# Local attention: the product taken turned, weights divided ahead of it, and new orders on all engines

## The chip, the cores and the metric

One core of one Trainium2 chip. The metric is the time of one execution in microseconds (us) on the device. The runs of the kernel before took 2020.76, 2023.39 and 2024.77 us, median 2023.39.

## What is computed

The input is 32 sequences of 256 tokens with 128 channels, all in fp32. A linear attention (16 heads of 8) comes first, with normalisation and residual. Then come two layers, each with a local attention and a gated feed-forward. The change touches only the local attention, of which this is the reference, cut to what matters:

```python
h = shift_token(x)                      # second half of the channels from the token before
q, k, v = split(h @ wqkv, 3)            # 8 heads of 64
q = l2norm(q) * qs;  k = l2norm(k) * ksc
q, k = rotary_xpos(q, k)                # t * cos + rotate_half(t) * sin, scaled
sim = einsum('bhwid,bhwjd->bhwij', bq, bk)      # windows of 64, each with the window before
attn = softmax(where(mask, -max, sim))
o = einsum('bhwij,bhwjd->bhwid', attn, bv)
x = x + o @ wo
```

## The kernel before

All of it is one program with an instruction list for each engine, and semaphores between them. Phases follow one another: the linear attention, then for each of two layers the local attention (`t_sync`, `t_pool`, `t_act`, `t_dve`, `t_pe`) and the feed-forward (`f_*`).

The local attention works on tiles of 128 tokens, two to a sequence, 64 in a layer. It is a software pipeline written out by hand. In a slot each engine goes once through its list of steps, and every step names the tile that it works on by its lag: `Tile(l, i, p, s, 2)` is the tile two slots back. So a slot takes in one new tile and works on four at a time (lags 0 to 3); `t_steps` runs the slots, the middle ones in a hardware loop of four slots. The order within a list is the order in the text at the end of each function. Engines run in order; between them `wait_ge` on the semaphores `T[...]` holds a step until its input is there, and `until` holds it until the buffer that it writes has been read.

The way of a tile before: TensorE turns h (L940), ScalarE copies it to hT (L745), TensorE projects k (L954), q (L976) and v (L946) into banks 6 and 7 in turn. VectorE forms the rotary parts of k from the bank (L666 to L669 `straight`, L657 to L664 `swapped`, which is two instructions of half a head each) and adds them (ka, L866). ScalarE copies q to SBUF (L779) and GpSimd does the same three steps for q there (L729, L730, L733). ScalarE squares q and k (L807, L809), VectorE sums the squares per head (ss, L888), and GpSimd raises them to the power -1/2 (`power`: ss L719, rr L722). VectorE multiplies k by it (krot, L856). TensorE turns qrot and krot, ScalarE copies qT and kT (L786, L800), TensorE forms the scores on top of a mask product (L1024 to L1042) in banks 0 and 1. VectorE takes the largest of each row and head (mx, L896) and makes the bias (nb, L900). ScalarE takes eight exponentials of 128x128 (L769), four for even heads (e = 0) and four for odd ones, with rr as scale. TensorE turns the weights (`turn_even`, `turn_odd`), VectorE and ScalarE copy them to pT (L847, L793). The product (`weigh`, L1005, L1006) holds the turned weights stationary, 128x64, and moves the values past them: 64 columns and a 65th of ones, which gives the sum of the weights. `divide` takes the reciprocal of that (L875) and multiplies (L878); TensorE turns the result (`turn_o`), ScalarE copies it to oT (L752), TensorE projects it (L962), VectorE adds the residual (L839). Half the values are wanted on the other 64 partitions, which SP brings there by a DMA (`early_values`, L697). SP also loads hs and yt and stores yn.

TensorE's four-part transposes all stand at L926, in the helper `turn`.

Of the kernel before, what the change touches and what calls it, by code (L numbers as in the profile page):

```python
# [18 lines left out]
ALU = mybir.AluOpType  # L19
# [3 lines left out]
P = 128  # L23
# [54 lines left out]
def build(nc, x, w_qkv, w_out, b_out, rf, wqkv, q_scale, k_scale, wo, ln_g, ln_b, w1, b1, w2, b2, out,  # L78
# [17 lines left out]
    with ExitStack() as ctx:  # L96
# [130 lines left out]
        N_SET = 4 + 1 + 4  # L227
# [31 lines left out]
        def sa(name, shape, dt=F32):  # L259
# [76 lines left out]
        vt = sb("vt", [P, 2, TPB, HEADS, DH + 1])  # L336
        ve = sb("ve", [P, 2, HEADS, DH + 1])
# [3 lines left out]
        pT = sb("pT", [P, 2, UH, P])  # L341
        rl = sb("rl", [P, 2, UH])
        ot = sb("ot", [P, TPB, INNER])
# [302 lines left out]
        class Tile:  # L646

            def __init__(self, l, i, p, s, lag):
                back, self.t = divmod(s - lag, 2)
                self.b = i + back  # L650
# [6 lines left out]
        def swapped(on, src, dst, l, a, t):  # L657

            s4 = src.rearrange("p (h c d) -> p h c d", c=2, d=DH // 2)
            d4 = dst.rearrange("p (h c d) -> p h c d", c=2, d=DH // 2)  # L660
            for c in range(2):
                sin = ltab[:, l, a + 1, t, 32 * c:32 * c + 32].unsqueeze(1).broadcast_to([P, HEADS, DH // 2])
                m = on.tensor_tensor(d4[:, :, c, :], s4[:, :, 1 - c, :], sin, ALU.mult)  # L663
            return m  # L664

        def straight(on, src, dst, l, a, t):  # L666
            cos = ltab[:, l, a, t, :].unsqueeze(1).broadcast_to([P, HEADS, DH])
            return on.tensor_tensor(dst.rearrange("p (h d) -> p h d", d=DH), src.rearrange("p (h d) -> p h d", d=DH),  # L668
                                    cos, ALU.mult)  # L669

        def t_sync(sp, l, i, p):
# [19 lines left out]
            def early_values(X):  # L691
# [3 lines left out]
                until(sp, T["o_ps"], 4 * X.n - 4)  # L695
# [8 lines left out]
            early_values(Tile(l, i, p, 0, 1))  # L704
# [4 lines left out]
            early_values(Tile(l, i, p, 1, 1))  # L709

        def t_pool(pool, l, i, p, s):

            def power(X):
# [7 lines left out]
                until(pool, T["po"], X.x - 3)  # L721
                nc.gpsimd.tensor_tensor(rr[:, r, :], ss[:, r, :], half_neg[:], ALU.pow).then_inc(T["rr"], 1)  # L722

            def rotate_q(X):
# [4 lines left out]
                swapped(nc.gpsimd, qraw[:, X.t, :], m2q[:], l, 0, X.t)  # L729
                straight(nc.gpsimd, qraw[:, X.t, :], m1q[:], l, 0, X.t).then_inc(T["qm"], 1)  # L730
# [3 lines left out]

            power(Tile(l, i, p, s, 1))
            rotate_q(Tile(l, i, p, s, 0))

        def t_act(act, l, i, p, s):

# [7 lines left out]
            def turned_o(X):  # L747
                if not X.live:
                    return
                act.wait_ge(T["oT_ps"], X.x + 1)  # L750
                until(act, T["w_ps"], X.x - 1)
                nc.scalar.copy(oT[:, X.t].rearrange("p j n -> p (j n)"), turn_bank(s, 0)[:]).then_inc(T["oT"], 1)  # L752

            def values(X):
                if not X.live:
                    return
                act.wait_ge(T["v_ps"], X.x + 1)
                until(act, T["o_ps"], 2 * X.x - 4)
                nc.scalar.copy(vt[:, X.p, X.t, :, 0:DH],
                               project_bank(s, 0)[:].rearrange("p (h d) -> p h d", d=DH)).then_inc(T["v"], 1)  # L760

            def exps(X, e):
# [4 lines left out]
                for j in range(UH):  # L767
# [6 lines left out]
            def queries(X):  # L774
                if not X.live:
                    return
                act.wait_ge(T["q_ps"], X.x + 1)
                until(act, T["qrot"], X.x - 1)
                nc.scalar.copy(qraw[:, X.t, :], project_bank(s, 2)[:]).then_inc(T["q"], 1)  # L779

            def turned_q(X):
                if not X.live:
                    return
                act.wait_ge(T["qT_ps"], X.x + 1)
                until(act, T["s_ps"], X.x - 1)
                nc.scalar.copy(qT[:, X.t].rearrange("p j n -> p (j n)"), turn_bank(s, 2)[:]).then_inc(T["qT"], 1)  # L786

            def turned_odd(X):
                if not X.live:
                    return  # L790
                act.wait_ge(T["po_ps"], X.x + 1)
                until(act, T["o_ps"], 2 * X.x)
                nc.scalar.copy(pT[:, 1].rearrange("p j n -> p (j n)"), turn_bank(s, 3)[:]).then_inc(T["pTo"], 1)  # L793

            def turned_k(X):
# [4 lines left out]
                nc.scalar.copy(kT[:, X.p, :, 1 - X.t, :], turn_bank(s, 4)[:].rearrange("p (j n) -> p j n", n=P)  # L800
                               ).then_inc(T["kT"], 1)

            def squares(X):
                if not X.live:
                    return
                until(act, T["ss"], X.x)
                nc.scalar.activation(sq[:, 0:INNER], project_bank(s, 2)[:], ACT.Square).then_inc(T["qs"], 1)  # L807
                act.wait_ge(T["km"], X.x + 1)
                nc.scalar.activation(sq[:, INNER:], project_bank(s, 1)[:], ACT.Square).then_inc(T["ks"], 1)  # L809
# [12 lines left out]
        def t_dve(dve, l, i, p, s):  # L822

            def rotate_k(X):
                if not X.live:
                    return
                dve.wait_ge(T["k_ps"], X.x + 1)
                until(dve, T["ka"], X.x)
                straight(nc.vector, project_bank(s, 1), m1k[:], l, 2, X.t)
                swapped(nc.vector, project_bank(s, 1), m2k[:], l, 2, X.t).then_inc(T["km"], 1)  # L830

            def residual(X):
                if not X.live:
                    return
                if X.t == 0:
                    dve.wait_ge(T[f"y_in{X.p}"], 16 * half_count(X.n))
                    until(dve, T[f"out{X.p}"], 16 * (half_count(X.n) - 1))
                dve.wait_ge(T["w_ps"], X.x + 1)
                nc.vector.tensor_tensor(yn[:, X.p, X.t, :], yt[:, X.p, X.t, :], bank[4][:, 0:D], ALU.add  # L839
                                        ).then_inc(T["yn"], 1)  # L840

            def turned_even(X):
                if not X.live:
                    return
                dve.wait_ge(T["pe_ps"], X.x + 1)
                until(dve, T["o_ps"], 2 * X.x - 1)
                nc.vector.tensor_copy(pT[:, 0].rearrange("p j n -> p (j n)"), turn_bank(s, 1)[:]  # L847
                                      ).then_inc(T["pTe"], 1)

            def norm_k(X):  # L850
                if not X.live:
                    return
                dve.wait_ge(T["rr"], X.x + 1)
                dve.wait_ge(T["ka"], X.x + 1)
                until(dve, T["kT_ps"], X.x - 1)
                nc.vector.tensor_tensor(krot[:, X.t, :].rearrange("p (h d) -> p h d", d=DH),  # L856
                                        ka[:].rearrange("p (h d) -> p h d", d=DH),
                                        rr[:, 2 * X.p + X.t, HEADS:].unsqueeze(2).broadcast_to([P, HEADS, DH]),
                                        ALU.mult).then_inc(T["krot"], 1)

            def add_k(X):
                if not X.live:
                    return
                dve.wait_ge(T["km"], X.x + 1)
                until(dve, T["krot"], X.x)
                nc.vector.tensor_tensor(ka[:], m1k[:], m2k[:], ALU.add).then_inc(T["ka"], 1)  # L866

            def divide(X):
                if not X.live:
                    return  # L870
                o = psA[2].rearrange("p (e n) -> p e n", e=2)[:, :, 0:UH * (DH + 1)].rearrange(
                    "p e (j d) -> p e j d", d=DH + 1)
                dve.wait_ge(T["o_ps"], 2 * X.x + 2)
                until(dve, T["o"], X.x)
                nc.vector.reciprocal(rl[:], o[:, :, :, DH]).then_inc(T["rl"], 1)  # L875
                dve.wait_ge(T["rl"], X.x + 1)
                until(dve, T["oT_ps"], X.x - 1)
                nc.vector.tensor_tensor(ot[:, X.t].rearrange("p (j e d) -> p e j d", e=2, d=DH), o[:, :, :, 0:DH],  # L878
# [501 lines left out]
```

## Time and profile before

| | |
|---|---|
| runs shown | 2020.76, 2023.39, 2024.77 us (median 2023.39) |
| the profiled execution, its own time | 2025.17 us |
| its span in the profile | 2023.4 us |
| mean granted TensorE clock | 0.98 |
| PE busy | 1821.6 us (90%) |
| DVE busy | 1387.1 us (69%) |
| ACT busy | 1290.3 us (64%) |
| POOL busy | 1207.2 us (60%) |

PE is TensorE (PEld its weight loads), DVE VectorE, ACT ScalarE, POOL GpSimd, SP the queue that issues the DMAs. An engine's busy time is what its instructions last; a PE at 90% isn't at its peak, since matmuls are pipelined. "L926" is line 926 of the kernel. What stands behind `<-` in brackets is what ended an idle time of the engine. A row with x2 and more merges that many instructions of one kind in a row. In a projection or a product each fp32 matmul shows as two.

### The profile page before, as it was taken

The numbers are of one execution on the slowest core, as the hardware profiler recorded it, in microseconds if no ns is written. First come the engines' busy times: TensorE is split into PE (matmuls) and PEld (weight loads), VectorE is DVE, ScalarE is ACT, GpSimd is POOL, SyncE is SP. The second block draws the span as 40 slices with busy tenths as digits, with TensorE's granted clock in tenths as the row PEclk, the third lists the DMA queues.
The fourth block names the chain that finished last, engine by engine and source line by source line (L and its number), as shares of the span: only waits on it lengthen the run. The fifth ranks groups of instructions, "written<-read, shape, count | busy, mean of one in ns | idle before, by whom it ended". The sixth has DMA issues, their size and how long they took to land.

```text
span 2023.4 us, 54270 instructions
## 1 busy us (share of the span) xinstructions
PE 1821.6 (90%) x18884; PEld 1223.0 (60%) x18884; DVE 1387.1 (69%) x3157; ACT 1290.3 (64%) x2692; POOL 1207.2 (60%) x1143
## 2 busy tenths in 40 slices
PE   4999999689999999999969988999999999996997
PEld 3666666356666666666635545666666666663554
DVE  3777777567777777777746746777777777774887
ACT  4888888467777777777732216777777777773221
POOL 0323323277777777777722217777777777773454
PEclk9999999899999999999989988999999999998999
DMA  4111111111111111111113221111111111112342
GB/s 100 53 49 44 51 48 46 50 30 36 36 34 34 31 38 35 31 34 32 35 46 82 78 60 30 36 32 37 36 31 34 31 39 34 31 32 53 98 113 81
DMA packets 209334, 94.31 MB, mean 47 GB/s; under 512 B 90818, under 2 KB 200300, under 8 KB 209260
## 3 DMA queue, kind: packets, MB, share of 16 engines
q1 hardware_dynamic: 209260, 93.35, 17.7%
q8 instruction: 43, 0.70, 0.1%
q14 instruction: 31, 0.25, 0.0%
HBM read 51.03 MB, written 25.23 MB: 38 GB/s over the span
## 4 chain that ended last, share of the span: by engine, by line
PE 56%; ACT 17%; issue 10%; POOL 4%; DVE 4%; SPq 4%; DMA 4%; ACTq 0%; POOLq 0%; DVEq 0%
PE banks L926 17%; ACT pr L769 8%; PE banks L976 5%; PE banks L946 5%; PE banks L1024 4%; ACT kT L800 4%; PE banks L1005 4%; DMA f_y<-y_d 3%; PE banks L561 3%; PE banks L510 3%; PE banks L1042 3%; PE banks L575 3%; SPq L1094 3%; PE banks L1034 2%; ACT L472 2%
## 5 line engine op out<-in xcount | busy, mean ns | idle before, releaser
L663 POOL TENSOR_TENSOR m2q<-qraw,ltab 128x256 f32<-128x256 f32 x256 | 244.7, 976 | 251.4 <-ACT qraw L779 229.3
L722 POOL TENSOR_TENSOR rr<-ss,half_neg 128x16 f32<-128x16 f32 x128 | 374.2, 2923 | 19.1 <-POOL ss L719 17.1
L769 ACT ACTIVATE pr<-banks,nb,rr 128x128 f32<-128x128 f32 x1024 | 371.7, 477 | 0.8 <-DVE nb L900 0.6
L926 PE MATMUL banks<-ident,pr 128*128 128x128 f32 x1024 | 161.4, 280 | 59.1 <-ACT pr L769 56.4
L1157 ACT ACTIVATE f_g<-banks,b_s 128x512 f32<-128x512 f32 (+1 forms) x96 | 65.8, 686 | 225.2 <-PE banks L1241 224.2
L888 DVE TENSOR_REDUCE ss<-sq 128x16 f32<-128x1024 f32 x128 | 156.1, 1220 | 30.8 <-ACT sq L809 27.9
L1006 PE MATMUL banks<-vt,pT 128*64 128x65 f32 x2048 | 173.9, 228 | 0.0
L962 PEld LDWEIGHTS banks<-wo_s,oT 128*128 128x128 f32 x1024 | 134.0, 192 | 63.2 <-issue 45.8
L733 POOL TENSOR_TENSOR qrot<-m1q,m2q 128x512 f32<-128x512 f32 x128 | 162.9, 1273 | 14.2 <-POOL m1q L668 8.2
L745 ACT COPY hT<-banks 128x128 f32<-128x128 f32 x128 | 34.0, 266 | 214.5 <-PE banks L940 214.5
L926 PEld LDWEIGHTS banks<-ident,pr 128*128 128x128 f32 x1024 | 113.7, 141 | 85.8 <-ACT pr L769 85.8
L668 POOL TENSOR_TENSOR m1q<-qraw,ltab 128x512 f32<-128x512 f32 x128 | 163.6, 1278 | 0.0
L372 POOL TENSOR_SCALAR a_ve<-a_mv 128x2 f32<-128x2 f32 x96 | 21.1, 220 | 231.4 <-DVE a_mv L383 228.4
L896 DVE TENSOR_REDUCE mx<-banks 128x8 f32<-128x1024 f32 x128 | 155.5, 1215 | 3.1 <-PE banks L1034 3.1
L875 DVE RECIPROCAL rl<-banks 128x8 f32<-128x8 f32 x128 | 26.6, 208 | 181.8 <-PE banks L1006 181.8
L1034 PE MATMUL banks<-kT,qT 64*64 64x128 f32 x2048 | 141.4, 278 | 0.0
L1006 PEld LDWEIGHTS banks<-vt,pT 128*64 128x64 f32 x2048 | 138.4, 137 | 0.0
L668 DVE TENSOR_TENSOR m1k<-banks,ltab 128x512 f32<-128x512 f32 x128 | 88.6, 692 | 72.2 <-PE banks L954 72.2
L962 PE MATMUL banks<-wo_s,oT 128*128 128x128 f32 x1024 | 135.5, 276 | 2.7 <-ACT oT L752 2.7
L946 PE MATMUL banks<-wqkv_s,hT 128*128 128x512 f32 x256 | 133.9, 605 | 3.0 <-ACT sq L809 3.0
L954 PE MATMUL banks<-wqkv_s,hT 128*128 128x512 f32 x256 | 134.3, 607 | 0.8 <-ACT hT L745 0.8
L847 DVE COPY pT<-banks 128x512 f32<-128x512 f32 x128 | 88.5, 692 | 67.4 <-PE banks L926 67.3
(130 smaller groups left out, 4677.0 us busy)
## 6 DMA issues: line engine op xcount, KB each, us to landing
ve<-vt SPq DMA_DIRECT2D x128, 130.0 KB, 2.2
hs<-y_d SPq DMA_DIRECT2D x128, 64.0 KB, 1.9
yt<-y_d SPq DMA_DIRECT2D x64, 128.0 KB, 2.1
y_d<-yn SPq DMA_DIRECT2D x64, 128.0 KB, 2.0
f_h<-y_d SPq DMA_DIRECT2D x128, 64.0 KB, 2.0
f_y<-y_d SPq DMA_DIRECT2D x64, 128.0 KB, 2.2
xa<-in_L_attn_x SPq DMA_DIRECT2D x32, 128.0 KB, 2.1
xr<-in_L_attn_x SPq DMA_DIRECT2D x32, 128.0 KB, 2.3
```

The source lines that it names most:

```text
L663: m = on.tensor_tensor(d4[:, :, c, :], s4[:, :, 1 - c, :], sin, ALU.mult)
L668: return on.tensor_tensor(dst.rearrange("p (h d) -> p h d", d=DH), src.rearrange("p (h d) -> p h d", d=DH), cos, ALU.mult)
L722: nc.gpsimd.tensor_tensor(rr[:, r, :], ss[:, r, :], half_neg[:], ALU.pow).then_inc(T["rr"], 1)
L733: nc.gpsimd.tensor_tensor(qrot[:, X.t, :], m1q[:], m2q[:], ALU.add).then_inc(T["qrot"], 1)
L769: a = nc.scalar.activation(pr[:, e, j, :], bank[e][:, j * P:(j + 1) * P], ACT.Exp, bias=nb[:, X.t, UH * e + j:UH * e + j + 1], scale=rr[:, ...
L888: nc.vector.tensor_reduce(ss[:, 2 * X.p + X.t, :], sq[:].rearrange("p (h d) -> p h d", d=DH), AX.X, ALU.add).then_inc(T["ss"], 1)
L896: nc.vector.tensor_reduce(mx[:], psA[0].rearrange("p (j k) -> p j k", k=P), AX.X, ALU.max).then_inc(T["mx"], 1)
L926: m = nc.tensor.transpose(b[:, j * P:(j + 1) * P], src[:, j * P:(j + 1) * P], ident[:])
L946: nc.tensor.matmul(project_bank(s, 0)[:], hT[:, X.t, :], wqkv_s[:, l, 2 * INNER:], start=True, stop=True).then_inc(T["v_ps"], 1)
L962: m = nc.tensor.matmul(bank[4][:, 0:D], oT[:, X.t, c, :], wo_s[:, l, c, :], start=(c == 0), stop=(c == 3))
L1006: m = nc.tensor.matmul(o[64:128], pT[:, e, j, 64:128], vt[:, X.p, X.t, h, :], start=True, stop=True)
L1034: m = nc.tensor.matmul(o, q, own, start=False, stop=True, skip_group_check=True)
```

## The change

The product is turned round: a tile's values are stationary (128x64) and the turned weights move, 64 columns at a time, so that the result has head and channel on the partitions and tokens on the columns, as the output projection wants it. `turn_o` and its copy go; ScalarE's `weighed` copies the product (bank 4) to oT. The column of ones goes, and with it two memsets at the start. The sum of the weights comes from the exponentials' `accum_out` (ls); VectorE's `share`, once for the odd and once for the even heads, takes its reciprocal (4 columns) and multiplies the weights (128x512 in SBUF) before they are turned. `swapped` is one instruction with a reversed read of the two half heads. The product and what follows it now have lags 3 and 4. The banks are fixed: 2 for turned weights, 3 for qT and kT, 4 the product, 5 for turned h and the output projection. All five lists have new orders; sums, squares_k, add_k and add_q move to the next slot.

```diff
-            nc.vector.memset(vt[:], 1.0).then_inc(set_done, 1)
-            nc.vector.memset(ve[:], 1.0).then_inc(set_done, 1)
...
         def swapped(on, src, dst, l, a, t):
-            s4 = src.rearrange("p (h c d) -> p h c d", c=2, d=DH // 2)
+            s4 = src.rearrange("p (h c d) -> p h c d", c=2, d=DH // 2)[:, :, ::-1, :]
             d4 = dst.rearrange("p (h c d) -> p h c d", c=2, d=DH // 2)
-            for c in range(2):
-                sin = ltab[:, l, a + 1, t, 32 * c:32 * c + 32].unsqueeze(1).broadcast_to([P, HEADS, DH // 2])
-                m = on.tensor_tensor(d4[:, :, c, :], s4[:, :, 1 - c, :], sin, ALU.mult)
-            return m
+            sin = ltab[:, l, a + 1, t, :].rearrange("p (c d) -> p c d", c=2).unsqueeze(1).broadcast_to(
+                [P, HEADS, 2, DH // 2])
+            return on.tensor_tensor(d4, s4, sin, ALU.mult)
...
             if held(i + 1):
                 load_h(i + 1, 1 - p)
-            early_values(Tile(l, i, p, 0, 1))
+            early_values(Tile(l, i, p, 0, 2))
+            early_values(Tile(l, i, p, 1, 2))
             if held(i):
                 load_y(i, p)
             if held(i - 2):
                 store(i - 2, p)
-            early_values(Tile(l, i, p, 1, 1))
...
+            add_q(Tile(l, i, p, s, 1))
             power(Tile(l, i, p, s, 1))
-            rotate_q(Tile(l, i, p, s, 0))
+            turned_parts(Tile(l, i, p, s, 0))
```

`add_q` is the sum of L733, `turned_parts` the two products of L729 and L730, straight first. ScalarE's list and its exponentials:

```diff
-                                             scale=rr[:, 2 * X.p + X.t, h:h + 1])
+                                             scale=rr[:, 2 * X.p + X.t, h:h + 1], accum_out=ls[:, e, j:j + 1])
...
-            turned_h(Tile(l, i, p, s, 0))
-            turned_o(Tile(l, i, p, s, 3))
-            values(Tile(l, i, p, s, 1))
-            exps(Tile(l, i, p, s, 2), 0)
-            exps(Tile(l, i, p, s, 2), 1)
-            queries(Tile(l, i, p, s, 0))
-            turned_q(Tile(l, i, p, s, 1))
-            turned_odd(Tile(l, i, p, s, 2))
-            turned_k(Tile(l, i, p, s, 1))
-            squares(Tile(l, i, p, s, 0))
+            squares_k(Tile(l, i, p, s, 1))
+            turned_h(Tile(l, i, p, s, 0))
+            values(Tile(l, i, p, s, 2))
+            weighed(Tile(l, i, p, s, 4))
+            turned_odd(Tile(l, i, p, s, 3))
+            queries(Tile(l, i, p, s, 0))
+            turned_q(Tile(l, i, p, s, 1))
+            exps(Tile(l, i, p, s, 2), 1)
+            exps(Tile(l, i, p, s, 2), 0)
+            turned_k(Tile(l, i, p, s, 1))
```

`queries` now squares q and then copies it. VectorE:

```diff
+            def share(X, e):
+                if not X.live:
+                    return
+                dve.wait_ge(T[("pe", "po")[e]], X.x + 1)
+                until(dve, T[("ne", "no")[e]], X.x)
+                nc.vector.reciprocal(rl[:, e], ls[:, e]).then_inc(T[("le", "lo")[e]], 1)
+                dve.wait_ge(T[("le", "lo")[e]], X.x + 1)
+                nc.vector.tensor_tensor(pr[:, e], pr[:, e], rl[:, e].unsqueeze(2).broadcast_to([P, UH, P]), ALU.mult
+                                        ).then_inc(T[("ne", "no")[e]], 1)
...
-            rotate_k(Tile(l, i, p, s, 0))
-            residual(Tile(l, i, p, s, 3))
-            turned_even(Tile(l, i, p, s, 2))
-            norm_k(Tile(l, i, p, s, 1))
-            add_k(Tile(l, i, p, s, 0))
-            divide(Tile(l, i, p, s, 2))
-            sums(Tile(l, i, p, s, 0))
-            peak(Tile(l, i, p, s, 1))
+            share(Tile(l, i, p, s, 3), 0)
+            sums(Tile(l, i, p, s, 1))
+            peak(Tile(l, i, p, s, 2))
+            add_k(Tile(l, i, p, s, 1))
+            minus_peak(Tile(l, i, p, s, 2))
+            turned_even(Tile(l, i, p, s, 3))
+            swapped_k(Tile(l, i, p, s, 0))
+            norm_k(Tile(l, i, p, s, 1))
+            share(Tile(l, i, p, s, 2), 1)
+            residual(Tile(l, i, p, s, 4))
+            straight_k(Tile(l, i, p, s, 0))
```

TensorE:

```diff
+                for j in range(UH):
+                    for w in range(2):
+                        for e in range(2):
+                            h = 2 * j + e
+                            early = vt[:, X.p, 0, h, :] if X.t == 0 else ve[:, X.p, h, :]
+                            m = nc.tensor.matmul(bank[4][64 * e:64 * e + 64, j * P + 64 * w:j * P + 64 * w + 64],
+                                                 vt[:, X.p, X.t, h, :] if w else early,
+                                                 pT[:, e, j, 64 * w:64 * w + 64], start=True, stop=True)
...
-            turn_o(Tile(l, i, p, s, 3))
-            turn_h(Tile(l, i, p, s, 0))
-            project_v(Tile(l, i, p, s, 1))
-            project_k(Tile(l, i, p, s, 0))
-            out_project(Tile(l, i, p, s, 3))
-            turn_even(Tile(l, i, p, s, 2))
-            project_q(Tile(l, i, p, s, 0))
-            turn_q(Tile(l, i, p, s, 1))
-            turn_odd(Tile(l, i, p, s, 2))
-            weigh(Tile(l, i, p, s, 2), 0)
-            turn_k(Tile(l, i, p, s, 1))
-            weigh(Tile(l, i, p, s, 2), 1)
-            scores(Tile(l, i, p, s, 1))
+            project_v(Tile(l, i, p, s, 2))
+            turn_h(Tile(l, i, p, s, 0))
+            turn_odd(Tile(l, i, p, s, 3))
+            scores(Tile(l, i, p, s, 2))
+            project_q(Tile(l, i, p, s, 0))
+            turn_q(Tile(l, i, p, s, 1))
+            turn_even(Tile(l, i, p, s, 3))
+            project_k(Tile(l, i, p, s, 0))
+            out_project(Tile(l, i, p, s, 4))
+            weigh(Tile(l, i, p, s, 3))
+            turn_k(Tile(l, i, p, s, 1))
```

## Rows read from the trace of the kernel before

**Rows 1.** Busy time in a stretch of the first local attention (us; busy, xcount; clock; DMA)

```profile
500.00:600.00 100.00, 94.57 (x1066) 65.59 (x1065) 71.75 (x124) 74.45 (x174) 79.10 (x63) 1.00 0.13 33
```

**Rows 2.** Turn_h (L940) on PE, slots 3 to 63 of the first stage: ns, starts us

```profile
L940 PE MATMUL banks<-ident,hs x61: 272/273/273, 425.9 to 1006.2; 128*128 128x128 f32 x61
```

**Rows 3.** Chain of waits in one steady slot: start us, us, what

```profile
913.53 0.86 PE banks L976 x2
914.39 0.88 PE banks L926 x8
915.26 0.20 PE banks L1005
...
915.88 0.60 PE banks L926 x4
...
917.22 0.60 PE banks L1024 x2
...
918.86 0.59 PE banks L926 x4
```

**Rows 4.** Timeline of ACT in a steady slot: start us, us, what

```profile
901.60 2.90 ACT L769 ACTIVATE pr<-banks,nb,rr 128x128 f32<-128x128 f32 x8
904.72 0.59 ACT L779 COPY qraw<-banks 128x512 f32<-128x512 f32 x1 [0.21 <-PE banks L976]
905.20 0.59 ACT L786 COPY qT<-banks 128x512 f32<-128x512 f32 x1
```

**Rows 5.** A one-column activation of the linear attention (L484): ns min/median/max

```profile
L484 ACT ACTIVATE a_exp<-half_neg x32: 202/203/203, 32.6 to 371.3; 128x1 f32<-128x1 f32 x32
```

**Rows 6.** Timeline of DVE, `divide` near the end of the first stage

```profile
1013.72 0.21 DVE L875 RECIPROCAL rl<-banks 128x8 f32<-128x8 f32 x1 [1.47 <-PE banks L1006]
1013.96 0.69 DVE L878 TENSOR_TENSOR ot<-banks,rl 128x512 f32<-128x512 f32 x1
```

**Rows 7.** Timeline of DVE and POOL in a steady slot

```profile
901.90 0.69 DVE L668 TENSOR_TENSOR m1k<-banks,ltab 128x512 f32<-128x512 f32 x1 [0.42 <-PE banks L954]
902.50 0.74 DVE L663 TENSOR_TENSOR m2k<-banks,ltab 128x256 f32<-128x256 f32 x2
...
905.36 0.69 DVE L866 TENSOR_TENSOR ka<-m1k,m2k 128x512 f32<-128x512 f32 x1
905.38 1.94 POOL L663 TENSOR_TENSOR m2q<-qraw,ltab 128x256 f32<-128x256 f32 x2 [1.70 <-ACT qraw L779]
907.28 1.27 POOL L668 TENSOR_TENSOR m1q<-qraw,ltab 128x512 f32<-128x512 f32 x1
...
908.64 1.22 DVE L888 TENSOR_REDUCE ss<-sq 128x16 f32<-128x1024 f32 x1
...
909.77 1.21 DVE L896 TENSOR_REDUCE mx<-banks 128x8 f32<-128x1024 f32 x1
910.05 0.25 POOL L719 TENSOR_SCALAR ss<-ss 128x16 f32<-128x16 f32 x1
910.46 2.92 POOL L722 TENSOR_TENSOR rr<-ss,half_neg 128x16 f32<-128x16 f32 x1 [0.16 <-POOL ss L719]
911.02 0.17 DVE L900 SCALAR_TENSOR_TENSOR nb<-mx,rr 128x8 f32<-128x8 f32 x1
```

**Rows 8.** Timeline of DVE and POOL at the start of the stage

```profile
406.72 2.92 POOL L722 TENSOR_TENSOR rr<-ss,half_neg 128x16 f32<-128x16 f32 x1
409.61 1.85 POOL L663 TENSOR_TENSOR m2q<-qraw,ltab 128x256 f32<-128x256 f32 x2
409.68 1.20 DVE L856 TENSOR_TENSOR krot<-ka,rr 128x512 f32<-128x512 f32 x1 [3.12 <-POOL rr L722]
410.98 1.03 DVE L866 TENSOR_TENSOR ka<-m1k,m2k 128x512 f32<-128x512 f32 x1
411.43 1.71 POOL L668 TENSOR_TENSOR m1q<-qraw,ltab 128x512 f32<-128x512 f32 x1
```

**Rows 9.** Krot (L856) over both stages: ns min/median/max

```profile
L856 DVE TENSOR_TENSOR krot<-ka,rr x128: 680/682/1200, 409.7 to 1832.8; 128x512 f32<-128x512 f32 x128
```

More of the change, by code:

```diff
@@ L649, in __init__ @@
                 back, self.t = divmod(s - lag, 2)
+                self.end = 2 * B * (l + 1)
                 self.b = i + back
@@ L669, in straight, with passed_tile @@
                                     cos, ALU.mult)
+        def passed_tile(eng, s, X, d):
+            v = X.x + d + 1
+            until(eng, s, min(v, X.end) if isinstance(v, int) else v)
         def t_sync(sp, l, i, p):
@@ L820, in t_act @@
-            squares(Tile(l, i, p, s, 0))
[L822 to L878, printed above, removed]
-                                        rl[:].unsqueeze(3).broadcast_to([P, 2, UH, DH]), ALU.mult
-                                        ).then_inc(T["o"], 1)
@@ L897, in peak, with add_k, minus_peak @@
                                         ).then_inc(T["mx"], 1)
+            def add_k(X):
+                if not X.live:
+                    return
+                dve.wait_ge(T["km"], X.x + 1)
+                until(dve, T["krot"], X.x)
+                nc.vector.tensor_tensor(ka[:], m1k[:], m2k[:], ALU.add).then_inc(T["ka"], 1)
+            def minus_peak(X):
+                if not X.live:
+                    return
                 dve.wait_ge(T["mx"], X.x + 1)
-                until(dve, T["po"], X.x - 1)
+                until(dve, T["pe"], X.x - 1)
                 nc.vector.scalar_tensor_tensor(
@@ new lines, in residual, with straight_k @@
+            def residual(X):
+                if not X.live:
+                    return
+                if X.t == 0:
+                    dve.wait_ge(T[f"y_in{X.p}"], 16 * half_count(X.n))
+                    until(dve, T[f"out{X.p}"], 16 * (half_count(X.n) - 1))
+                dve.wait_ge(T["w_ps"], X.x + 1)
+                nc.vector.tensor_tensor(yn[:, X.p, X.t, :], yt[:, X.p, X.t, :], bank[5][:, 0:D], ALU.add
+                                        ).then_inc(T["yn"], 1)
+            def straight_k(X):
+                if not X.live:
+                    return
+                straight(nc.vector, k_bank(X), m1k[:], l, 2, X.t).then_inc(T["km"], 1)
@@ L1042, in scores, with project_q, turn_q @@
                                 nc.tensor.matmul(o, q, both, start=False, stop=True, skip_group_check=True)
-            turn_o(Tile(l, i, p, s, 3))
+            def project_q(X):
+                if not X.live:
+                    return
+                pe.wait_ge(T["hT"], X.x + 1)
+                until(pe, T["ks"], X.x)
+                nc.tensor.matmul(q_bank(X)[:], hT[:, X.t, :], wqkv_s[:, l, 0:INNER],
+                                 start=True, stop=True).then_inc(T["q_ps"], 1)
+            def turn_q(X):
+                if not X.live:
+                    return
+                pe.wait_ge(T["qrot"], X.x + 1)
+                until(pe, T["kT"], X.x)
+                turn(qrot[:, X.t], bank[3], T["qT_ps"])
@@ new lines, in turn_even, with project_k @@
+            def turn_even(X):
+                if not X.live:
+                    return
+                pe.wait_ge(T["ne"], X.x + 1)
+                pe.wait_ge(T["pTo"], X.x + 1)
+                turn(pr[:, 0].rearrange("p j n -> p (j n)"), bank[2], T["pe_ps"])
+            def project_k(X):
+                if not X.live:
+                    return
+                until(pe, T["v"], X.x - 1)
+                nc.tensor.matmul(k_bank(X)[:], hT[:, X.t, :], wqkv_s[:, l, INNER:2 * INNER],
+                                 start=True, stop=True).then_inc(T["k_ps"], 1)
@@ new lines, in out_project @@
+            def out_project(X):
+                if not X.live:
+                    return
+                pe.wait_ge(T["oT"], X.x + 1)
+                passed_tile(pe, T["hT"], X, 4)
+                if isinstance(X.x, int) and X.x + 4 >= X.end:
+                    pe.wait_ge(T["yn"], X.x)
+                for c in range(4):
+                    m = nc.tensor.matmul(bank[5][:, 0:D], oT[:, X.t, c, :], wo_s[:, l, c, :],
+                                         start=(c == 0), stop=(c == 3))
+                m.then_inc(T["w_ps"], 1)
```

211 lines of the change are left out of this document (97 added, 114 removed), and 3 rows, old and new, of the table T.

## The prediction

> **What bounds the kernel now.** I read the table by stretches first, then the chain of waits of a few steady slots, then the instructions of the two engines that the change loads. The local attention is two stages, one per layer; in them TensorE is recorded busy 94.5%, GpSimd 79%, ScalarE 74%, VectorE 72% [rows 1]. Nothing else of the program changes, so the whole question is the length of a slot (one 128-token tile; each engine goes once through its list). turn_h runs once per slot: 61 of them start from 425.9 to 1006.2, which is 580.3/60 = **9.67 us a slot** [rows 2]. In the chain the slot is almost only TensorE: a projection 0.86, two turns 0.87, the scores from 917.22 to the next turn at 918.86, 1.64, and so on, with ScalarE in it twice (first four exponentials, copy of kT) [rows 3]. VectorE and GpSimd have two to three us of slack each.
>
> **TensorE, part by part.** Removed: turning the divided output, four transposes, 0.44 (half of 0.87) [rows 3]. The product has the same 16 matmuls, 64 columns in place of 65, in one group instead of two: one change of array form less, some 0.17, taken from the chain, where the turn of krot after the first group (0.62 long, 915.26 to 915.88) is given 0.60, against 0.44 each for two turns in a row [rows 3]. What is left: 3 projections 2.6, four turns 1.75, turn_h 0.1, scores 1.6, output projection 0.9 (512 columns in all, as the others), product 1.1: **8.0 us**. If TensorE were still the bound, this alone would be 1.6 us a slot. It loses that place, see below.
>
> **ScalarE.** Eight 512-column passes stay eight (the copy of turned o becomes the copy of the product). They are 0.48 apart (904.72, 905.20) and the eight exponentials take 2.90 [rows 4], 2.76 apart plus the last one's tail; with hT 0.17 that makes 6.8. New: each exponential also gives its sum. No row shows that. Below, 0. Above, a whole one-column instruction each: 203 ns [rows 5]. Nearest is that instruction overlapped as its neighbours are (0.59 long, 0.48 apart), so 0.1 each, 0.8 a slot: 7.6. Covered in my forecast by a 9.8 us slot; without that cover it counts in full (first rival).
>
> **VectorE.** Out go one reciprocal and one multiply. In come two reciprocals of 4 columns and two multiplies of 128x512 with both inputs in SBUF. A reciprocal is 0.21 and its multiply starts 0.24 after it [rows 6]; a 512-column pass is 0.69 long and 0.60 after its predecessor (901.90, 902.50) [rows 7]. The two swapped halves (0.74 together) become one reversed 0.69: from -0.1 to, if a reversed read ran at half speed, +0.6; VectorE waits for rr right behind it, so the small end is hidden by that wait. Sum: seven passes 4.2, two reductions 2.26 (1.13 apart), two reciprocals 0.48, residual and nb 0.3, 7.3 to 7.6. That fits too.
>
> **What decides: the pair of engines.** A GpSimd and a VectorE operation that both read two SBUF tensors exclude each other. Steady state now: ka starts at 905.36, ends 906.05, and the first m2q, issued 905.38, makes two m2q take 1.94 instead of 1.44 [rows 7]. Much more telling is the start of the stage [rows 8]. rr (406.72) ends at 409.64. GpSimd's own next instruction starts at 409.61; krot, which waited for rr, starts at 409.68 and takes 1.20 instead of 0.68: it ends 0.55 after the first m2q would end (409.61+0.72 = 410.33). The second m2q is then stopped until krot is done, ka until m2q is done, and m1q (411.43, 1.71 long) ends 1.13 after ka (412.01). So they alternate, and behind rr GpSimd wins. In the steady slot today krot starts when GpSimd is idle, and only this start-up has it: the median krot is 682 ns, the longest 1200 [rows 9]. In the new lists it is every slot. GpSimd runs add_q, power, turned_parts. Counted from the krot before: turn_k, project_v, turn_h, turn_odd, scores and project_q end 4.6 us after it, square and copy of q 5.8 after it, rr 8.0 after it (9.8 less term (c) below). So q is there in time, and m1q starts the moment rr ends. And krot must now wait for rr, because sums moved from late in one slot to early in the next, with only mx, ka, nb, turned_even and swapped_k (3.0 us from the end of sums' own 1.13) to cover what GpSimd needs (to 4.7 from sums' start, against 4.2).
>
> Ring of one slot, from the start of straight_k (new lists, old durations):
> (a) straight_k 0.60, reciprocal 0.24, even share 0.60 = 1.44; ScalarE's square beside it needs 0.69+0.08+0.60+0.10 = 1.47: **1.49** with a short wait for qrot.
> (b) sums 1.22, at most 0.19 to GpSimd (909.86 to 910.05), 0.41 from ss to rr (910.05, 910.46), 2.89 from rr to the next (406.72, 409.61) [rows 7, 8]: **4.71**.
> (c) m1q 1.27, krot ends 0.55 later: **1.82**.
> (d) odd reciprocal and share: ready 0.15 after krot, but m2q, one 512-column pass of 1.27, has the pair; it ends 1.13 after krot, the share 0.55 after that: **1.68**.
> (e) residual, then straight_k again starts 0.11 after the share's end.
> Sum 9.81, against 9.67: **+0.14 to +0.16 a slot**. TensorE (8.0), ScalarE (7.6) and the DMAs have from 0.3 to 2 us of slack against every point of it. 128 slots less fill, say 124 at 0.16: +20 us. The pipeline is one tile deeper (lag 4 for lag 3), and the added end slot holds little work: +2 us a layer, +4. SP's early-value loads go one slot later and two are issued together, still a slot ahead of their reader: 0; if that slot were not there, the product of every second tile would wait for them. The two memsets removed write 3120 columns in the set-up, ahead of VectorE's wait for the weights' DMAs: 0; without that cover a gain of some 3.7 us, at the 0.60 per 512 columns of a pass [rows 7]. Together +24. Against the profiled execution's 2025.2 that is 2049; it lies 1.8 above the median of the runs shown, so I predict **2047**. Uncertain inside this case: term (d) by the reversed read on GpSimd (0.1 less to 0.3 more), the others by 0.05 each. Its own range is 2020 to 2085.
>
> A rule is weighed here. The row: nb, two SBUF inputs, starts at 911.02 while rr (910.46, 2.92) runs, and takes its usual 0.17 [rows 7]. So I let ka run beside rr. The Trainium skill ("SBUF — State Buffer", section "SBUF: two separate sides") says that whichever of the two engines' operations starts first has the shared ports for the whole instruction. It is a rival below.
>
> **Rivals.**
> 1. *Faster: the pair does not cost what the start-up shows.* If krot got in first behind rr, its stall (1.27+0.55 against 0.69) goes: 9.81-1.13 = 8.7, 2025+4-124x0.97 = 1909. If nothing collided, the next ring is scores 1.57, project_q 1.02, square, q and qT copies 1.44, exponentials 2.76 plus their sums, kT 0.59, hand-overs 0.17: 7.55 without the sums' cost, 8.35 at 0.1 each, 9.15 at 0.2. That gives 1963 to 1822 (TensorE's 8.0 is the floor), 1865 in the middle. For it: busy times alone all say so. Against: the start of the stage, where GpSimd won by 0.07 [rows 8]. Chance 0.20 (0.08 and 0.12). A further 0.06 for the ring itself below 9.6, between 1985 and 2019.
> 2. *No change:* the ring at 9.62 to 9.68: 0.07.
> 3. *Slower by much: the reversed read.* m2q is now two 256-element forms, 0.72 each. If the reversed form costs GpSimd between nothing and a second pass (1.27), each 0.1 is 12 us: at 0.5, 2110; at 1.27, over 2200. It decides from 0.3 on. Chance 0.07.
> 4. *rr holds the pair all its 2.92 us.* Then ka, due 2.3 us into (b), waits until rr ends 2.4 later, and krot comes after it, into m2q: about 11.4 a slot, 2240. The 0.17 of nb speaks against it [rows 7]. Chance 0.03. (It is what the section of the Trainium skill named above says in full; that nb is not held disagrees with it.)
> *The change does not do what it says:* if the product's two halves (even and odd heads) did not run side by side, it would add 0.9 to TensorE (8.9): hidden at 9.8, some 1934 in rival 1.
>
> **How the numbers follow.** The ring has 0.57 and sets 2047. Faster by over 0.2% (about 4 us, what this kernel's measurement can tell): 0.20+0.06 = 0.26; within: 0.07; slower: 0.57+0.07+0.03 = 0.67. The range 1905 to 2100 leaves out the collision-free case (0.12) and the far ends of rivals 3 and 4 (0.05).
>
> **What would show it.** krot near 1.75 us in every slot and the odd share near 1.5, both with GpSimd's m1q and m2q beside them; m2q near 1.7 (1.27 plus the wait for krot); VectorE waiting some 0.4 for rr ahead of krot; turn_k and with it all of TensorE waiting for krot, TensorE's busy share down; slots of 9.8. Wrong if krot stays at 0.68, if turn_h starts come every 8.3 to 8.7, or if the unhindered m2q is not 1.27. An exponential with its sum longer than 0.45 apart would matter only in the faster cases.

## The result and the profile after

The runs of the changed kernel took 2039.1 to 2041.08 us, median **2040.56**; the kernel before took 2023.19 beside it. The ratio is **1.0087** (95% interval 1.0075 to 1.0099): slower by 17.4 us, which is under 1% but clear of the noise. The forecast was 2047, slower. The profiled execution has a span of 2038.3 us at a mean granted clock of 0.98, as before.

The same stretch as in [rows 1], with the same columns (PE, PEld, DVE, ACT, POOL):

```profile
500.00:600.00 100.00, 86.08 (x966) 58.91 (x977) 94.14 (x134) 79.10 (x252) 77.86 (x51) 1.00 0.13 33
```

TensorE fell from 94.6% to 86.1% at the same clock. VectorE rose from 72% to 94%, which looks like a new bound; the experiments show that about a fifth of it is waiting recorded as work. Turn_h (now L961), against [rows 2]:

```profile
L961 PE MATMUL banks<-ident,hs x60: 272/328/329, 431.6 to 1013.4; 128*128 128x128 f32 x60
```

581.8/59 = **9.86 us a slot**, +0.19 against 9.67. The timeline of VectorE and GpSimd in a steady slot, against [rows 7]:

```profile
901.42 1.27 POOL L667 TENSOR_TENSOR m1q<-qraw,ltab 128x512 f32<-128x512 f32 x1
901.57 1.66 DVE L910 TENSOR_TENSOR krot<-ka,rr 128x512 f32<-128x512 f32 x1 [0.49 <-POOL rr L727]
902.64 1.72 POOL L663 TENSOR_TENSOR m2q<-qraw,ltab 128x512 f32<-128x512 f32 x1
...
903.35 1.56 DVE L853 TENSOR_TENSOR pr<-pr,rl 128x512 f32<-128x512 f32 x1
904.44 1.60 POOL L742 TENSOR_TENSOR qrot<-m1q,m2q 128x512 f32<-128x512 f32 x1
...
905.03 0.68 DVE L667 TENSOR_TENSOR m1k<-banks,ltab 128x512 f32<-128x512 f32 x1
...
905.83 0.76 DVE L853 TENSOR_TENSOR pr<-pr,rl 128x512 f32<-128x512 f32 x1
906.61 1.22 DVE L862 TENSOR_REDUCE ss<-sq 128x16 f32<-128x1024 f32 x1
...
908.45 2.93 POOL L727 TENSOR_TENSOR rr<-ss,half_neg 128x16 f32<-128x16 f32 x1 [0.17 <-POOL ss L724]
908.88 0.68 DVE L878 TENSOR_TENSOR ka<-m1k,m2k 128x512 f32<-128x512 f32 x1
...
911.35 1.27 POOL L667 TENSOR_TENSOR m1q<-qraw,ltab 128x512 f32<-128x512 f32 x1
```

The collisions alternate. m1q starts 0.15 ahead of krot and ends at 902.69; krot ends 0.54 later, at 903.23. m2q, issued meanwhile, has to let krot go first and ends at 904.36. The odd share waits for it and ends 0.55 later, at 904.91. Krot over both stages (ns min/median/max; what VectorE waited for before it; who waited for it), against [rows 9]:

```profile
L910 DVE TENSOR_TENSOR krot<-ka,rr x128: 692/1750/1767, 409.9 to 1849.3; 128x512 f32<-128x512 f32 x128
its engine sat idle before it (us, times) until:
  POOL rr L727: 53.4, 125
who waited for it (us, times):
  PEld banks L946: 149.3, 128
```

The chain of waits of the whole run has 18% on rr, where TensorE had 56% before. In one steady slot (start, us, what), against [rows 3]:

```profile
898.53 2.92 POOL rr L727
...
901.63 1.52 issue
...
903.89 0.94 issue
904.84 0.27 DVE yn L922
905.11 0.62 DVE m1k L667
...
905.83 0.61 ACT sq L767
...
906.61 1.23 DVE ss L862
...
908.47 2.92 POOL rr L727
```

TensorE isn't in it. The 1.52 and 0.94 of "issue" are krot and the odd share while stopped: no semaphore is involved, so the view has no releaser for them.

**By stage.** From the first turn_h to the last yn the two layers took 637.6 and 640.6 us before, 647.5 and 647.1 after: +9.9 and +6.5. The rest of the span changes by -1.5, together +14.9, the difference of the spans. In parts, where the fill is the time from the first to the fourth turn_h, the steady part the 60 distances after it, and the drain the time from the last turn_h to the last yn (us, before to after):

| | fill | steady part | drain |
|---|---|---|---|
| first layer | 28.7 to 23.8, **-4.9** | 580.4 to 591.5, +11.1 | 28.5 to 32.2, +3.7 |
| second layer | 31.9 to 23.7, **-8.2** | 580.2 to 592.8, +12.6 | 28.5 to 30.6, +2.1 |

### The profile page after: what moved, and what is told of

It reads as the page before. It is cut to its first block, busy times and chain, and to the rows that moved or that the text cites. A ratio compares the mean times of both kernels' runs of the same rounds, so it can differ in the third digit from the quotient of the medians.

```text
span 2038.3 us, 54605 instructions
## 1 busy us (share of the span) xinstructions
PE 1734.1 (85%) x18244; PEld 1156.1 (57%) x18372; DVE 1675.4 (82%) x3283; ACT 1367.8 (67%) x3716; POOL 1215.0 (60%) x1015
## 4 chain that ended last, share of the span: by engine, by line
issue 25%; POOL 23%; DVE 21%; PE 15%; ACT 7%; SPq 4%; DMA 4%; DVEq 1%; POOLq 1%; ACTq 0%
POOL rr L727 18%; DVE ss L862 7%; DVE m1k L667 4%; PE banks L560 3%; DVE pr L853 3%; DMA f_y<-y_d 3%; PE banks L509 3%; PE banks L574 3%; SPq L1109 3%; ACT L471 2%; PE banks L500 2%; POOL f_yb L1154 2%; DVE yn L922 2%; POOL ss L724 2%; ACT qf L467 2%
## 5 line engine op out<-in xcount | busy, mean ns | idle before, releaser
L820 ACT ACTIVATE pr<-banks,nb,rr 128x128 f32<-128x128 f32 x1024 | 455.9, 491 | 6.1 <-DVE nb L885 6.1
L853 DVE TENSOR_TENSOR pr<-pr,rl 128x512 f32<-128x512 f32 x256 | 293.2, 1145 | 8.8
L910 DVE TENSOR_TENSOR krot<-ka,rr 128x512 f32<-128x512 f32 x128 | 216.5, 1692 | 53.4 <-POOL rr L727 53.4
L820 ACT ACTIVATION_READ_ACCUMULATOR pr<-banks,nb,rr 128x1 f32 x1024 | 244.0, 238 | 0.0
L663 POOL TENSOR_TENSOR m2q<-qraw,ltab 128x512 f32<-128x512 f32 x128 | 219.9, 1718 | 0.0
L946 PE MATMUL banks<-ident,krot 128*128 128x128 f32 x512 | 84.2, 287 | 127.7 <-DVE krot L910 127.7
L767 ACT ACTIVATE sq<-banks 128x512 f32<-128x512 f32 x128 | 76.6, 598 | 142.0 <-DVE m1k L667 142.0
L1001 PE MATMUL banks<-wqkv_s,hT 128*128 128x512 f32 x256 | 146.7, 655 | 5.1 <-ACT hT L774 5.1
L1049 PE MATMUL banks<-pT,vt 128*64 128x64 f32 x3072 | 137.5, 224 | 1.3 <-DVE pT L895 1.3
L946 PEld LDWEIGHTS banks<-ident,krot 128*128 128x128 f32 x512 | 53.6, 140 | 149.3 <-DVE krot L910 149.3
```

Source lines behind the costliest of these rows:

```text
L663: return on.tensor_tensor(d4, s4, sin, ALU.mult)
L820: a = nc.scalar.activation(pr[:, e, j, :], bank[e][:, j * P:(j + 1) * P], ACT.Exp, bias=nb[:, X.t, UH * e + j:UH * e + j + 1], scale=rr[:, ...
L853: nc.vector.tensor_tensor(pr[:, e], pr[:, e], rl[:, e].unsqueeze(2).broadcast_to([P, UH, P]), ALU.mult).then_inc(T[("ne", "no")[e]], 1)
L946: m = nc.tensor.transpose(b[:, j * P:(j + 1) * P], src[:, j * P:(j + 1) * P], ident[:])
L1001: nc.tensor.matmul(q_bank(X)[:], hT[:, X.t, :], wqkv_s[:, l, 0:INNER], start=True, stop=True).then_inc(T["q_ps"], 1)
```

## The experiments

Three theories. **One** (the prediction's): the slot is set by a ring, a chain of waits that closes on itself one slot later, through rr, krot and the odd share, and what lengthens it are the stops between VectorE and GpSimd instructions that read two SBUF tensors. **Two**: VectorE, 94% busy, is simply full; only less work on it helps. **Three**: rr comes too late because sums moved, and the stops are incidental. The slots below are distances of turn_h in the first stage; ratios are to the kernel before. The expectations call the versions e1 to e10, in the order below.

**Krot ahead of m1q.** GpSimd waits for krot, then begins q's products.

```diff
                 until(pool, T["qrot"], X.x)
+                until(pool, T["krot"], X.x)
                 straight(nc.gpsimd, qraw[:, X.t, :], m1q[:], l, 0, X.t)
```

> Edit: GpSimd's turned_parts also waits for krot of the tile before, so krot meets no running GpSimd operation; nothing else changes. Theory 1 (the ring through rr, krot, odd share, with the collisions in it): krot back to 0.69, its stall of about 1.05 goes, the odd share is still held, now by m1q; slot 9.0 in place of 9.86, time 1930 (1915 to 1950). Theory 2 (VectorE is simply full: it has the same work as before, 94% busy): no gain, 2035 to 2060, since only a wait is added. Theory 3 (rr comes late, collisions are incidental): the wait for rr stays, little changes, 2020 to 2045.

Measured: 1994.95 us, ratio 0.986 (0.983 to 0.989), slot 9.53. Timeline of VectorE and GpSimd:

```profile
901.24 0.69 DVE L911 TENSOR_TENSOR krot<-ka,rr 128x512 f32<-128x512 f32 x1 [1.12 <-POOL rr L727]
902.05 0.69 DVE L854 TENSOR_TENSOR pr<-pr,rl 128x512 f32<-128x512 f32 x1
902.10 1.79 POOL L667 TENSOR_TENSOR m1q<-qraw,ltab 128x512 f32<-128x512 f32 x1 [0.99 <-DVE krot L911]
...
903.84 1.73 POOL L663 TENSOR_TENSOR m2q<-qraw,ltab 128x512 f32<-128x512 f32 x1
...
906.70 0.76 DVE L879 TENSOR_TENSOR ka<-m1k,m2k 128x512 f32<-128x512 f32 x1
906.88 0.69 POOL L724 TENSOR_SCALAR ss<-ss 128x16 f32<-128x16 f32 x1
```

VectorE does the same work in 80.6% of the time in place of 94.1%, and the kernel is faster with a wait more: theory two falls. But no theory's range holds the 1995 us: theory one expected 9.0 a slot, and the gain is 0.33 where it had 0.86. VectorE now wins, and GpSimd is stopped: m1q by 0.52, m2q by 0.46, ss by 0.44. GpSimd's list has no free time but the 0.9 to 1.0 that it waits for krot, and has become the ring: 902.10 to the next m1q at 911.56.

**The odd heads' reciprocals in PSUM.** The reciprocals of the odd heads go to a free part of bank 5, so the multiply has one SBUF input (turn_h waits for its reader). Cut to what matters:

```diff
+                by = rl[:, e]
+                if e == 1:
+                    until(dve, T["w_ps"], X.x - 1)
+                    passed_tile(dve, T["hT"], X, 2)
+                    by = bank[5][:, 256:256 + UH]
...
```

> Edit: the odd heads' reciprocals go to PSUM (bank 5), so the odd share reads one SBUF tensor and can't collide; krot and the even share are as in the changed kernel. Theory 1: the odd share falls from 1.56 to 0.69, but the even share then arrives while GpSimd's qrot has the pair and gives most of it back (its length grows from 0.76 to about 1.3); slot 9.55 to 9.65, time 2005 (1995 to 2020). Theory 2: no gain, 2035 to 2050. A theory that sums the collisions one by one: 0.84 less a slot, 1935.

Measured: 2000.59 us, ratio 0.989 (0.986 to 0.992), slot 9.51.

```profile
905.30 0.69 DVE L858 TENSOR_TENSOR pr<-pr,banks 128x512 f32<-128x512 f32 x1
906.90 1.30 DVE L858 TENSOR_TENSOR pr<-pr,rl 128x512 f32<-128x512 f32 x1
```

The odd share is 0.69 in place of 1.56, and krot is 1.66 as it was. But the even share, earlier now, meets qrot and takes 1.30 in place of 0.76: 0.54 of the 0.87 goes back.

**Krot with its factor in PSUM.** VectorE copies rr's 8 columns to bank 5, and krot reads them there. Again turn_h waits until bank 5 is free; cut to what matters:

```diff
+                rk = bank[5][:, 264:264 + HEADS]
+                nc.vector.tensor_copy(rk, rr[:, 2 * X.p + X.t, HEADS:]).then_inc(T["rk"], 1)
+                dve.wait_ge(T["rk"], X.x + 1)
...
-                                        rr[:, 2 * X.p + X.t, HEADS:].unsqueeze(2).broadcast_to([P, HEADS, DH]),
+                                        rk.unsqueeze(2).broadcast_to([P, HEADS, DH]),
```

> Edit: VectorE copies rr's eight columns to PSUM ahead of krot, so krot reads one SBUF tensor and can't collide; one small VectorE instruction and a wait on it are added. The shares are as in the changed kernel. Theory 1: krot 0.69 again, the odd share waits only for the rest of m1q, the even share falls after or between GpSimd's three passes; the ring is no longer the longest; slot 8.3, set by ScalarE's list and TensorE, time 1845 (1830 to 1890). Theory 2: slower by the added copy, 2045 to 2070. Theory 3: 2020 to 2045.

Measured: 1915.13 us, ratio 0.946 (0.944 to 0.949), slot 8.86 on average, of two kinds in turn:

```profile
904.27 0.69 DVE L915 TENSOR_TENSOR krot<-ka,banks 128x512 f32<-128x512 f32 x1
904.98 1.28 POOL L663 TENSOR_TENSOR m2q<-qraw,ltab 128x512 f32<-128x512 f32 x1
905.08 1.73 DVE L853 TENSOR_TENSOR pr<-pr,rl 128x512 f32<-128x512 f32 x1
...
914.29 0.69 DVE L853 TENSOR_TENSOR pr<-pr,rl 128x512 f32<-128x512 f32 x1
914.36 1.76 POOL L663 TENSOR_TENSOR m2q<-qraw,ltab 128x512 f32<-128x512 f32 x1
```

This adds an instruction to VectorE and takes 125 us off. A lead of 0.10 or 0.07 us decides the race between m2q and the odd share, and the loser waits for the whole of the other. In the trace slots of 9.23 take turns with slots of 8.44 and 8.55 (distances of turn_h). The short kind is near the expected 8.3, the long kind, where m2q wins, is not, and the time is over the expected range of 1830 to 1890.

**Both factors in PSUM.**

> Both edits: neither krot nor the odd share can collide. Theory 1 with the alternation of the two engines: slower than e3 although less can collide, because the even share now comes just behind the start of GpSimd's qrot and waits for all of it, inside the ring; slot 8.95, time 1928 (1910 to 1945). A theory in which each collision taken away is a gain: not slower than e3, 1845 or less. Theory 2: 2045 to 2070.

Measured: 1939.1 us, ratio 0.958 (0.955 to 0.962), slot 9.07: slower than with krot's alone, as expected. The even share is stopped by qrot:

```profile
909.15 1.27 POOL L742 TENSOR_TENSOR qrot<-m1q,m2q 128x512 f32<-128x512 f32 x1 [0.16 <-POOL m2q L663]
909.26 1.71 DVE L858 TENSOR_TENSOR pr<-pr,rl 128x512 f32<-128x512 f32 x1
```

So the stops are not a sum of prices, one for each pair; to take one away moves the next.

**The race decided.** Krot's factor in PSUM, and m2q waits for the odd share.

```diff
                 straight(nc.gpsimd, qraw[:, X.t, :], m1q[:], l, 0, X.t)
+                until(pool, T["no"], X.x - 1)
                 swapped(nc.gpsimd, qraw[:, X.t, :], m2q[:], l, 0, X.t).then_inc(T["qm"], 1)
```

> Edit: e3 (krot can't collide), and GpSimd's m2q also waits for the odd share of the tile before. In e3 the slots come in two lengths: the odd share is ready some 0.1 us after m1q ends, and in one kind of slot GpSimd's m2q has just started and it waits 1.05 for it. Theory 1 (who has started first decides, and it decides the slot): with the added wait all slots are of the short kind, 8.3 to 8.45, set by ScalarE and TensorE; time 1850 (1835 to 1875). A theory in which e3's 8.86 is VectorE's or GpSimd's plain work: an added wait on GpSimd gains nothing, 1910 to 1930.

Measured: 1872.23 us, ratio 0.925 (0.924 to 0.927), slot 8.49. GpSimd now waits 0.82 for the share and the kernel gains 43 us:

```profile
904.63 1.28 POOL L663 TENSOR_TENSOR m2q<-qraw,ltab 128x512 f32<-128x512 f32 x1 [0.82 <-DVE pr L854]
```

All odd shares take 0.69, the even one 0.99. From 440 to 860 us all slots are now between 8.38 and 8.68; the long kind is gone. The race was the cause of the long kind, that is of 0.37 of the 0.56 by which the 8.86 lay over the expected 8.3.

**The power in two halves.** K's 8 columns first, so that krot can start while GpSimd does q's (nb, which needs q's, waits for the second half):

```diff
-                nc.gpsimd.tensor_tensor(rr[:, r, :], ss[:, r, :], half_neg[:], ALU.pow).then_inc(T["rr"], 1)
+                nc.gpsimd.tensor_tensor(rr[:, r, HEADS:], ss[:, r, HEADS:], half_neg[:, HEADS:], ALU.pow
+                                        ).then_inc(T["rr"], 1)
+                nc.gpsimd.tensor_tensor(rr[:, r, 0:HEADS], ss[:, r, 0:HEADS], half_neg[:, 0:HEADS], ALU.pow
+                                        ).then_inc(T["rq"], 1)
```

> Edit of the changed kernel, SBUF operands as they are: the power is taken in two instructions, eight columns for k first (krot waits for these alone), then eight for q (nb of the next slot waits for them). Theory 1: krot and the odd share run under the second power, which does not hold them as rr did not hold ka; they are 0.69 each again, the ring through rr gets 1.3 shorter and free of collisions, and the next bound is GpSimd's own list with ScalarE's and TensorE's, 8.4 to 8.6 a slot, although GpSimd gets more work (two powers of about 1.65 for one of 2.92); time 1863 (1845 to 1890). Theory 2 (VectorE is full): its work is the same, 2035 to 2045. If a power held the shared pair, krot would wait 1.65 and the time would be near or over the changed kernel's, 2020 to 2080.

Measured: 1873.72 us, ratio 0.927 (0.925 to 0.929), slot 8.52.

```profile
898.53 1.66 POOL L727 TENSOR_TENSOR rr<-ss,half_neg 128x8 f32<-128x8 f32 x1 [0.16 <-POOL ss L724]
900.15 1.64 POOL L729 TENSOR_TENSOR rr<-ss,half_neg 128x8 f32<-128x8 f32 x1
900.99 0.68 DVE L914 TENSOR_TENSOR krot<-ka,rr 128x512 f32<-128x512 f32 x1
902.24 1.33 DVE L856 TENSOR_TENSOR pr<-pr,rl 128x512 f32<-128x512 f32 x1
```

Krot runs at 0.68 beside the second half and starts no later than VectorE's list allows. The two halves cost GpSimd 3.22 where one took 2.89 to the next instruction, and it gained 167 us. Krot still has two SBUF inputs and VectorE the same list, so it speaks for theory one and against two. The odd share is still stopped (1.33). Theory three has a part in it, since this edit both makes rr earlier for krot and takes krot's stop away, and does not part the two. But the PSUM runs gain with rr 2.9 long, 8.49 a slot in the last of them: what rr's lateness did was to set krot against m1q. Sums in its old place was not run.

**The same split in the kernel before.**

> The kernel before with the same split of the power. Theory 1: nothing there hangs on rr in time (TensorE's list sets the 9.67 us slot), so no change, 2018 to 2028. If the wait for rr or a collision behind it had been in the old ring as well, it would gain as e6 does.

Measured: 2015.66 us, ratio 0.996 (0.995 to 0.998); slot 9.68, unchanged, as theory one has it, since krot does not wait there. No change at all was expected (2018 to 2028), and the gain (6.4 us by the medians, 8.1 by the spans) is at the fills: from the first to the last turn_h the stages take 606.1 and 607.9 us in place of 609.1 and 612.1, and of these 3.0 and 4.2 us the fills alone give 2.6 and 4.1. The fill is the place of [rows 8].

**The single reversed read in the kernel before.**

> The kernel before with one part of the change alone: one instruction with a reversed read in place of two, on VectorE and GpSimd. All theories: TensorE's list sets the slot, no change, 2018 to 2028; the trace gives the price of a reversed read: 0.69 on VectorE and 1.27 on GpSimd if it costs nothing, GpSimd's first pass longer by the wait for ka (1.8).

Measured: 2023.67 us, ratio 1.0005 (0.9995 to 1.0014), slot 9.68. The columns are ns min/median/max:

```profile
L663 DVE TENSOR_TENSOR m2k<-banks,ltab x128: 680/681/683, 401.3 to 1821.5; 128x512 f32<-128x512 f32 x128
L663 POOL TENSOR_TENSOR m2q<-qraw,ltab x128: 1260/1798/1802, 402.5 to 1824.3; 128x512 f32<-128x512 f32 x128
```

The reversed read costs neither engine anything: GpSimd's shortest is 1.26, as m1q's; its median holds the stop by ka that it had before [rows 7].

**Split power and the odd reciprocals in PSUM.**

> Edit: e6 and the odd heads' reciprocals in PSUM as in e2, so the odd share can't collide (in e6 it still takes 1.34). Theory 1: in e6 the ring now runs from the odd exponentials over the odd share, the residual, turn_h, turn_odd, scores, project_q and ScalarE's copies back to the exponentials, 8.45, with the share's collision of 0.65 in it; without it the slot is ScalarE's 8.3, unless the even share takes the collision over; time 1850 (1838 to 1866). If e6 is bound by GpSimd's list (94% busy), nothing is gained, 1868 to 1880.

Measured: **1856.56 us**, ratio 0.917 (0.915 to 0.918), slot 8.36: the fastest version that computes all of the reference, 8.3% under the kernel before and 9% under the changed one.

```profile
500.00:600.00 100.00, 97.74 (x1152) 69.81 (x1163) 89.44 (x156) 91.97 (x300) 90.75 (x73) 1.00 0.16 39
```

```profile
901.58 0.68 DVE L919 TENSOR_TENSOR krot<-ka,rr 128x512 f32<-128x512 f32 x1
902.82 0.69 DVE L861 TENSOR_TENSOR pr<-pr,banks 128x512 f32<-128x512 f32 x1
904.58 0.69 DVE L861 TENSOR_TENSOR pr<-pr,rl 128x512 f32<-128x512 f32 x1
```

No VectorE instruction is stopped; GpSimd's qrot still is (1.5 to 1.8 in place of 1.27). VectorE is at 89% although it does 18% more slots (9.86/8.36) in the stretch than in the changed kernel at 94%. TensorE is at 97.7%, above the 94.6% of before [rows 1].

**Split power without the sums.** The exponentials write no `accum_out`, and ls is set to 1 once: this version leaves out the sums of the weights, so the weights are not divided by them.

> Edit: e6 without the sums of the exponentials (ls is set to one once, so the weights are not divided by their sums). It prices accum_out where ScalarE has little slack: four of the eight sums lie in e6's ring, 0.09 each. Theory 1: 0.3 to 0.35 less a slot, unless GpSimd's list takes over near 8.3; time 1840 (1828 to 1858). If e6 is bound by GpSimd's or VectorE's list, no change, 1868 to 1880.

Measured: 1854.62 us, ratio 0.916 (0.915 to 0.918), slot 8.39: 0.13 a slot under the split alone, against the 0.7 that ScalarE is freed of and the 0.3 to 0.35 expected. It is not a clean price of the sums, because the stops move too: the odd share falls from 1.33 to 0.69 and the median first half of rr grows from 1.67 to 2.01. In the stretch from 500 to 600 GpSimd is then the fullest but TensorE, 96.6%.

## Why the prediction was right

The sign and the mechanism held, and the size roughly: +17.4 us measured, +24 forecast. In part that is luck, since two errors of opposite sign partly cancel. Between the spans, +14.9 in all, the steady slots give +23.7 (forecast +20), fill and drain -7.3 (forecast +4), and the rest of the program -1.5 (forecast 0).

- **The ring.** In the slot from 905.03 the terms are: (a) 1.58 (1.49 forecast), through ScalarE's square; (b) 4.74 to m1q (4.71); (c) krot's end 1.81 after m1q's start (1.82); (d) the odd share's end, one slot earlier, 1.68 after krot's (1.68); (e) 0.12 (0.11). Sum 9.93, a little above the mean slot of 9.86; 9.81 was forecast. The two prices of the collision, 0.55 and 1.13, came from one start-up event [rows 8] and were right for 128 slots. The experiments show that the stops are the cause: with krot and the odd share free the slot is 9.07, with the even share down to 0.99 too it is 8.49, and with all of VectorE free, and the power split, 8.36.
- **Fill and drain**, +4 forecast: the term that was mis-sized. The drains are 3.7 and 2.1 longer, somewhat more than forecast, but the fills are 4.9 and 8.2 shorter: -7.3 in all. The step failed by counting a deeper pipeline as a longer end alone; the first slots were never worked out in the new order. The split power makes the fills of the kernel before 2.6 and 4.1 us shorter, so rr is on the path there. Beyond that the fill was not looked into.
- **TensorE** did give way: it is out of the chain and waits for krot. The 8.0 a slot is not shown: its recorded busy time in a slot is 8.5 in the changed kernel (86.08% of 9.86) and 8.2 in the fastest version (97.74% of 8.36), and no run came under 8.36.
- **ScalarE.** 0.1 a sum was taken between 0 and 0.2. The row of one exponential and the start of the next (columns as in the timelines):

```profile
900.54 0.48 ACT L820 ACTIVATE pr<-banks,nb,rr 128x128 f32<-128x128 f32 x1
900.88 0.23 ACT L820 ACTIVATION_READ_ACCUMULATOR pr<-banks,nb,rr 128x1 f32 x1
900.97 0.48 ACT L820 ACTIVATE pr<-banks,nb,rr 128x128 f32<-128x128 f32 x1
```

Starts are 0.43 apart, 0.09 more than the 0.34 before. It is an instruction of its own, mostly overlapped.
- **Rival 1, faster.** It didn't happen, but its price could be tested, and was too kind. Krot first was to give 8.7. The run with krot first gives 9.53; it has an added wait, so it is not quite the rival's case, but it shows that the 1.13 counted only krot's stall and not what GpSimd is stopped for in return. No collision was to give 8.35; with every VectorE instruction free it is 8.36, so this number held, but it takes two edits, one of which also makes rr earlier. What sets the 8.36 was not looked into further.
- **Rival 3.** The reversed read is free, on both engines.
- **Rival 4.** ka (908.88) runs its usual 0.68 inside rr (908.45 to 911.38). The rule of the Trainium skill ("SBUF — State Buffer", section "SBUF: two separate sides") is that the operation that starts first keeps the shared ports for all its length. For 512-column instructions the races above agree, to 0.05 us (902.05 against 902.10 with krot first); for the power the measurement does not, and the slot it would give, 11.4, did not come.
- The memsets at nothing, and SP's loads at nothing: the first turn_h is 1.0 us later than before (398.1 for 397.1), but in the versions of the changed kernel it lies anywhere from 396.3 to 398.3, so this says nothing; and no slot waits for the early values in the list of waits. Neither was tested alone.

## What to carry to other kernels

When work moves between engines' lists, write down for each instruction with two SBUF inputs on VectorE what GpSimd runs beside it; a start-up event in the old trace may show the price that the new order pays in every slot. Such a stop is recorded as busy time and as "issue" in the chain, so a VectorE at 94% may have a fifth of it to give (here stops of 1.07, 0.87 and 0.07 in a slot of 9.86): compare an instruction's median with its minimum before calling the engine full. Give one input of the critical instruction from PSUM, or split the long instruction ahead of it so that the order of starts is certain; expect the next pair to collide, and look again.

## What was not expected of the hardware

- **The power is stopped at its start, not later, and stops nobody after that.** In the version without sums the first half of rr starts at the same time as ka and takes 2.21 in place of 1.65; the second half, with krot beside it, is undisturbed.

```profile
899.66 0.68 DVE L882 TENSOR_TENSOR ka<-m1k,m2k 128x512 f32<-128x512 f32 x1
899.66 2.21 POOL L728 TENSOR_TENSOR rr<-ss,half_neg 128x8 f32<-128x8 f32 x1
901.84 1.63 POOL L730 TENSOR_TENSOR rr<-ss,half_neg 128x8 f32<-128x8 f32 x1
902.01 0.68 DVE L915 TENSOR_TENSOR krot<-ka,rr 128x512 f32<-128x512 f32 x1
```

The added 0.56 is about what is left of ka. In the traces of all the versions together, none of the ka, krot and shares that started over 0.06 us into a power took longer than 0.70 beside it; the few that started 0.02 to 0.05 into it took 0.70 to 0.74. So the power holds VectorE for less than 0.1 us at its start. Why is not shown.
- **Waiting counts.** A GpSimd instruction issued right behind another does not keep VectorE out: m2q follows m1q at once, but krot, already stopped, goes first. The medians over all tiles of the changed kernel (krot 1750 ns, m2q 1724 ns) say that this is the rule there. Between two that have both not started, the first start decides: in the traces of all the versions there are 626 pairs of a ka, krot or share and an m1q, m2q or qrot with starts less than 0.07 us apart, and in each the one that started later was stopped.
- **On GpSimd's side one SBUF input is enough.** GpSimd's ss reads one tensor. In the run with krot ahead of m1q it starts while ka runs and takes 0.69 in place of 0.25.
- **A factor in PSUM is enough.** A copy of 8 columns (0.17) takes the 1.07 stop out of krot, though its large input and its output stay in SBUF.
